# Layer 1 of a four-layer graph network: messages split into a float32r rounding and a remainder, summed by two products per tile

## The reference, cut to what matters

```python
h = jnp.concatenate([x[row], edge_attr], axis=1)
h = jax.nn.relu(h @ W1 + b1) @ W2 + b2
agg = scatter_mean(h, col, dim_size=x.shape[0])
z = jnp.concatenate([x, agg, u[batch]], axis=1)
return jax.nn.relu(z @ W3 + b3) @ W4 + b4
```

## Time and profile before

| | |
|---|---|
| median of three runs | 6288.9 us (6285.21, 6288.9, 6297.36) |
| span of the profiled execution | 6290.0 us; it comes with no time of its own beside the span |
| PE busy over the span | 4549.5 us, 72% |
| DVE, ACT, POOL busy | 2674.4, 1822.6, 3113.1 us |
| gathers of layer 1 | 1612, the first at 873 us, the last at 3245.36 us |

### The profile page before, as it was taken

One profiled execution on the slowest core, in us unless ns is written; L12 is line 12 of the kernel. 1 busy time (PEld: TensorE's weight loads), 2 busy tenths in 40 slices (PEclk: granted clock), 3 DMA queues, 4 the chain that ended last, 5 costly groups with the idle time before them and its releaser, 6 DMA issues.

```text
span 6290.0 us, 72860 instructions
## 1 busy us (share of the span) xinstructions
PE 4549.5 (72%) x24017; PEld 3664.1 (58%) x24017; DVE 2674.4 (43%) x9938; ACT 1822.6 (29%) x3934; POOL 3113.1 (49%) x3324
## 2 busy tenths in 40 slices
PE   6999978888888898888989995344444444544445
PEld 5888855666666566666669994234444343434334
DVE  8999943333333333333335442233333333333334
ACT  5888842222222222222224552011111111111112
POOL 0000036666666666666640004666666666666663
PEclk9999989999999999999999997666666666666667
DMA  6777765555555555555647784122222222222221
GB/s 152 166 163 167 164 162 178 178 179 177 180 176 179 179 177 179 179 179 177 182 133 220 244 243 112 44 48 48 47 47 48 49 48 47 47 50 48 48 48 29
DMA packets 473053, 804.93 MB, mean 128 GB/s; under 512 B 73183, under 2 KB 301706, under 8 KB 462698
## 3 DMA queue, kind: packets, MB, share of 16 engines
q0 software_dynamic: 140192, 443.73, 28.3%
q1 hardware_dynamic: 318378, 346.76, 18.1%
q10 hardware_dynamic: 14112, 9.74, 0.5%
HBM read 663.72 MB, written 136.22 MB: 127 GB/s over the span
## 4 chain that ended last, share of the span: by engine, by line
PE 47%; another core or an unknown queue 25%; DVE 12%; issue 11%; DMA 2%; ACT 2%; POOL 1%; DVEq 0%; ACTq 0%
PE bank L1034 12%; PE bank L1021 10%; PE bank L1205 7%; PE bank L689 5%; PE bank L669 3%; PE bank L1523 2%; DVE ring L987 2%; DVE ring L1415 2%; DMA atab<-at 2%; PE bank L1487 1%; PE bank L590 1%; POOL ring L550 1%; DVE hs L638 1%; PE bank L970 1%
## 5 line engine op out<-in xcount | busy, mean ns | idle before, releaser
L550 POOL DMA_INDIRECT ring<-ptab,src x1612 | 1526.9, 947 | 854.7 <-issue 446.2
L550 POOL DMA_INDIRECT ring<-htab,src x1612 | 1526.5, 947 | 853.1 <-issue 448.3
L1034 PE MATMUL bank<-ring,oh 128*126 128x384 f32 x3224 | 1257.8, 506 | 30.8 <-issue 30.3
L987 DVE TENSOR_TENSOR ring<-bank,ring 128x512 f32<-128x512 f32 x806 | 543.0, 687 | 1613.4 <-remote 855.2
L1021 PE MATMUL bank<-w1e,ea 128*128 128x256 f32 x3224 | 892.4, 400 | 252.2 <-DVE ring L987 190.9
L1021 PEld LDWEIGHTS bank<-w1e,ea 128*128 128x128 f32 x3224 | 620.1, 199 | 541.1 <-issue 270.9
L1523 PE MATMUL bank<-ring,oh 128*126 128x132 f32 x3224 | 675.6, 357 | 337.0 <-DVE ring L1415 224.6
L1003 ACT ACTIVATE ring<-ring 128x1024 f32<-128x1024 f32 x403 | 425.6, 1056 | 1400.5 <-DVE ring L987 1112.6
L1523 PEld LDWEIGHTS bank<-ring,oh 128*126 128x126 f32 x3224 | 583.5, 252 | 424.0 <-issue 219.9
L1034 PEld LDWEIGHTS bank<-ring,oh 128*126 128x126 f32 x3224 | 624.7, 196 | 290.5 <-issue 74.8
L689 PE MATMUL bank<-xhl,at 128*126 128x258 f32 x3822 | 712.6, 323 | 0.0
(11 more groups left out here) (268 smaller groups left out, 4727.0 us busy)
## 6 DMA issues: line engine op xcount, KB each, us to landing
atab<-at POOLq DMA_DIRECT2D x78, 1543.5 KB, 9.9
ring<-ea_r SPq DMA_DIRECT2D x403, 256.0 KB
ea<-ea_t SPq DMA_DIRECT2D x403, 256.0 KB
adjb<-atab SPq DMA_DIRECT2D x156, 535.5 KB, 4.6
adjb<-atab SPq DMA_DIRECT2D x78, 472.5 KB, 4.5
ring<-ptab,src POOLq DMA_INDIRECT x1612
ring<-htab,src POOLq DMA_INDIRECT x1612
ptab<-pO ACTq DMA_DIRECT2D x49, 128.0 KB, 7.3
```

The lines of the kernel that those rows point to most:

```text
L550: return e.indirect_dma_start(o, None, table, bass.IndirectOffsetOnAxis(ap=src[:, t:t + 1], axis=0))
L987: e.tensor_tensor(group1(gi, m % 2), MLP[m % 3][:, :].rearrange("p (g f) -> p g f", g=2), group1(gi, m % 2), ALU.add).then_inc(s_edge, 1)
L1034: w = e.matmul(SUM[s % 2][0:SL, 0:384], slots_of(s, i), rv1[:, t // G % NR1, t % G, :], start=i == 0, stop=t == END[s])
```

## The change

Between ACT's relu and PE's sums stands a new double buffer `halves1` (two groups of 4 x 2 x 384, float32r). ACT writes the relu of the group's rows into its first half, rounded to float32r by the write, and then copies the attributes the same way (`rows_high`, two instructions; it waits for `s_sum1` of group `gi - 2`, which frees the buffer). DVE then writes the remainders: `max(row, 0)` minus the rounding over 128x1024, and attributes minus rounding over 128x512 (`rows_rest`, at `q = 4 gi + 10`). PE sums each tile by two float32r products of 384 columns, with the same stationary slots (now written as float32r). The gathered ring is no longer read by PE: POOL and SP wait for DVE's second remainder (`s_rest1`) instead of `s_sum1`, and the ring has six groups instead of nine. At the end of a set ACT writes the rounding straight from the bank and DVE one subtraction, instead of ACT's scaling and DVE's three steps. The other edits move tensors: layer 3's ring and layer 0's `at0` get places of their own, and `oh` is declared float32r and read as float32 where it was.

```diff
-    NR1 = 9
+    NR1 = 6
+    NH1 = 2
     NR3 = 4
-    RING = max(NR3 * GT * HROW, NR1 * G * 384)
...
+            rv1 = sb("ring1", [P, NR1, G, 384], c=l1)
             ea = sb("ea", [P, NEA, G, P], c=l1)
+            halves1 = sb("halves1", [P, NH1, G, 2, 384], FR, c=l1)
             held1 = sb("held1", [P, NK, 2, 384], FR, c=l1)
-            over1 = sb("over1", [P, 2, 384], c=l1)
...
                 for gi in range(NG):
                     if gi >= NR1:
-                        e.wait_ge(s_sum1, G * (gi - NR1 + 1))
+                        e.wait_ge(s_rest1, 2 * (gi - NR1 + 1))
                     for j in range(G):
...
-            def sums_scaled(e, s):
+            def sums_upper(e, s):
                 e.wait_ge(s_sum1, END[s] + 1)
-                if s >= 2:
-                    e.wait_ge(s_kept1, 3 * s - 4)
-                e.activation(over1[0:SL, s % 2, :], SUM[s % 2][0:SL, 0:384], ACT.Copy, bias=0.0, scale=SPLIT).then_inc(
-                    s_scaled1, 1)
-
-            def sums_kept(e, s):
-
-                o, u, hi, lo = SUM[s % 2][0:SL, 0:384], over1[0:SL, s % 2, :], held1[0:SL, s % NK, 0, :], held1[0:SL, s % NK, 1, :]
-                e.wait_ge(s_scaled1, s + 1)
-                e.tensor_tensor(u, u, o, ALU.subtract).then_inc(s_kept1, 1)
-                e.wait_ge(s_kept1, 3 * s + 1)
                 if s >= NK:
                     e.wait_ge(s_add1, B1[s - NK] + 1)
-                e.scalar_tensor_tensor(out=hi, in0=o, scalar=SPLIT, in1=u, op0=ALU.mult, op1=ALU.subtract).then_inc(s_kept1, 1)
-                e.wait_ge(s_kept1, 3 * s + 2)
-                e.tensor_tensor(lo, o, hi.bitcast(F32), ALU.subtract).then_inc(s_kept1, 1)
+                e.activation(held1[0:SL, s % NK, 0, :], SUM[s % 2][0:SL, 0:384], ACT.Copy).then_inc(s_upper1, 1)
+
+            def sums_kept(e, s):
+
+                e.wait_ge(s_upper1, s + 1)
+                e.tensor_tensor(held1[0:SL, s % NK, 1, :], SUM[s % 2][0:SL, 0:384], held1[0:SL, s % NK, 0, :].bitcast(F32),
+                                ALU.subtract).then_inc(s_kept1, 1)
...
+            def halves_of(gi, h):
+                return halves1[:, gi % NH1, :, h, 0:256], halves1[:, gi % NH1, :, h, 256:384]
+
+            def rows_high(e, gi):
+
+                v, r = halves_of(gi, 0)
+                e.wait_ge(s_edge, 2 * gi + 2)
+                if gi >= NH1:
+                    e.wait_ge(s_sum1, G * (gi - NH1 + 1))
+                e.activation(v, group1(gi), ACT.Relu).then_inc(s_high1, 1)
+                e.wait_ge(s_ea[gi % NR1], 16 * (gi // NR1 + 1))
+                e.activation(r, rv1[:, gi % NR1, :, 256:384], ACT.Copy).then_inc(s_high1, 1)
+
+            def rows_rest(e, gi):
+
+                (v, r), (vh, rh) = halves_of(gi, 1), halves_of(gi, 0)
+                e.wait_ge(s_high1, 2 * gi + 1)
+                e.scalar_tensor_tensor(out=v, in0=group1(gi), scalar=0.0, in1=vh.bitcast(F32), op0=ALU.max,
+                                       op1=ALU.subtract).then_inc(s_rest1, 1)
+                e.wait_ge(s_high1, 2 * gi + 2)
+                e.tensor_tensor(r, rv1[:, gi % NR1, :, 256:384], rh.bitcast(F32), ALU.subtract).then_inc(s_rest1, 1)
...
+                    gi = q // G - 2
+                    if 0 <= gi < NG and q % G == 2:
+                        rows_rest(e, gi)
...
-                        e.wait_ge(s_edge, 2 * gi + 2)
-                        e.activation(group1(gi), group1(gi), ACT.Relu).then_inc(s_relu, 1)
+                        rows_high(e, gi)
                     if q in KEEPS1:
-                        sums_scaled(e, KEEPS1[q])
+                        sums_upper(e, KEEPS1[q])
...
-                            e.wait_ge(s_relu, t // G + 1)
-                            e.wait_ge(s_ea[t // G % NR1], 16 * (t // G // NR1 + 1))
+                            e.wait_ge(s_rest1, 2 * (t // G) + 2)
                         if i == 0:
                             e.wait_ge(s_oh1, s + 1)
                             if s >= 2:
-                                e.wait_ge(s_kept1, 3 * (s - 1))
-                        w = e.matmul(SUM[s % 2][0:SL, 0:384], slots_of(s, i), rv1[:, t // G % NR1, t % G, :], start=i == 0,
-                                     stop=t == END[s])
+                                e.wait_ge(s_kept1, s - 1)
+                        for h in range(2):
+                            w = e.matmul(SUM[s % 2][0:SL, 0:384], slots_r(s, i), halves1[:, t // G % NH1, t % G, h, :],
+                                         start=i == 0 and h == 0, stop=t == END[s] and h == 1)
```

More of the change, by code:

```diff
@@ L229, in slots_of, with slots_r @@
         def slots_of(s, i):
+            return ohf[:, s % 2, SL * i:SL * i + SL]
+        def slots_r(s, i):
             return oh[:, s % 2, SL * i:SL * i + SL]
@@ L491, in expected @@
             s_ptab, s_htab, s_out = (sem(f"s_{n}") for n in ("ptab", "htab", "out"))
-            s_mlp, s_edge, s_relu = (sem(f"s_{n}") for n in ("mlp", "edge", "relu"))
+            s_mlp, s_edge, s_high1, s_rest1 = (sem(f"s_{n}") for n in ("mlp", "edge", "high1", "rest1"))
             l1 = ExitStack()
+            rv1 = sb("ring1", [P, NR1, G, 384], c=l1)
             ea = sb("ea", [P, NEA, G, P], c=l1)
+            halves1 = sb("halves1", [P, NH1, G, 2, 384], FR, c=l1)
             held1 = sb("held1", [P, NK, 2, 384], FR, c=l1)
-            over1 = sb("over1", [P, 2, 384], c=l1)
             l1.close()
@@ L528, in expected @@
             halves2.close()
-            def view(n, w):
-                return ring[:, 0:n * G * w].rearrange("p (n g f) -> p n g f", n=n, g=G)
-            rv1 = view(NR1, 384)
             hbf = hflat.bitcast(BF)
@@ L1538, in any_order @@
             D.sem_inc(s_tick, 16)
+            ring = sb("ring", [P, 2320])
             one = Serial(s_tick, s_own, s_idle)
```

22 lines of the change are left out of this document (11 added, 11 removed).

## The result

The kernel after takes 6452.7 us (median of four runs, 6441.8 to 6459.15) against 6293.13 us for the kernel before on the same chip (four runs, 6285.21 to 6299.78): ratio 1.0252, 95% interval [1.0235, 1.0269]. It is slower, by half of what was forecast (+160 us against +300). The profiled execution has a span of 6455.9 us.

A forecast was written before the change was run, and what follows sets the result against it. Layer 1 was taken as bound by POOL's gathers and their pauses for PE's held increments, not by PE. 6290.0 + 323 (pauses) - 22 (fill and drain) = 6591, given as 6590 us; range 6260 to 6780.

The forecast's parts named there:

- POOL and held increments bound layer 1, not PE: Layer 1: PE's increments are held while gathers run; POOL's pauses, 153 of 2.50 us, let them out.
- The change of credit is what costs: Layer 1's ring: POOL waiting for DVE's second remainder lengthens its pauses; the term that counts, +323 us.
- DVE must first do the edge add (0.69), the two remainders (1.20 + 0.69): Layer 1: DVE's work between held increments' arrival and POOL's restart, at least 2.6 us more per pause.
- I take the middle of the first two, +323 us: Layer 1 pauses: between bursts staying at 9.9 gathers (+421 us) and growing to 13.3 (+225 us), both with the short chain.
- grow in full: Layer 1, short chain: bursts reach 13.3 gathers, 121 pauses of 4.79 us, +225 us.
- POOL is stopped by remainders: Layer 1 rival: gathers stand still 1.20 us per group; 7070 us, half hidden 6830; chance 0.12 shared with slow clock.
- likeliest case: Whole kernel: the forecast's main case, slower at 6590 us, own range 6490 to 6720, chance 0.62.
- Faster rival, float32 passes: Layer 1: holding is tied to PE's float32 passes, so fewer free the increments; 5913 us, chance 0.14 whole or in part.
- PE's sums 0.3 us per tile: PE's sums in layer 1: estimated cadence gain of 0.3 us per tile, valued at nothing in the steady state.
- ACT's new wait for the sums of group gi - 2, "nothing": ACT in layer 1: the wait is on a held increment, but due earlier than the `s_mlp` it stands behind; nothing.
- Fill and drain, -22: Start and end of layer 1: ring of six ends the first stream earlier, -12 us; cheaper sums after last gather, -10 us.
- Layers 0, 2, 3 and DVE's load: nothing: Moved tensors add no instruction in layers 0, 2, 3, 0 us; DVE, some 1370 of 2240 us busy, is no bound.

The follow-up runs named there:

- e4: Kernel after with layer 1's gathers replaced by contiguous loads from SP, so rows are of wrong sources; 5402.3 us (one run).
- e7: Kernel before with layer 1's gathers replaced by contiguous loads from SP, so rows are of wrong sources; 5839.1 us (one run).
- e8: Kernel after with PE summing only the rounded half by one float32 product, remainders made but not summed; 6472.1 us, ratio 1.0277.
- e9: Kernel after with POOL and SP waiting for PE's sums of group gi - 6 instead of DVE's second remainder; 6313.1 us, ratio 1.0034.
- e13: Kernel after with remainders replaced by one-input reductions behind the same waits, PE summing the rounding alone; 6532.0 us, ratio 1.0364.
- e5: Kernel before plus one DVE instruction per group reading two SBUF inputs, that nothing waits for; 6295.0 us, ratio 1.0008.
- e15: Kernel after without making or summing remainders, POOL and SP waiting for PE's sums of group gi - 6; 6256.0 us, ratio 0.9935.
- e6: Kernel before plus one DVE reduction per group reading one SBUF input, that nothing waits for; 6297.5 us, ratio 1.0018.
- e2: Kernel after with the first remainder as a plain tensor_tensor subtraction without the maximum, wrong for negative rows; 6441.9 us, ratio 1.0236.
- e3: Kernel after with relu in place, one rounding copy and one subtraction, each of 4 x 384 columns; 6372.9 us, ratio 1.0134.

## Why the prediction was right, and where its size was off

- *POOL and held increments bound layer 1, not PE:* right. Without gathers no increment is late and PE binds (e4, e7); with them 437 us of PE's work shrink to 20 us (e8).
- *The change of credit is what costs:* right. One edit takes back 87% of the loss (e9). POOL's pauses are released by DVE's second remainder, as forecast, and went from 2.50 to 5.65 us; forecast was 2.50 + 2.6 = 5.1.
- *"DVE must first do the edge add (0.69), the two remainders (1.20 + 0.69)":* the wrong link. The increment that is waited for is not the edge add's `s_mlp` but the sums' `s_sum1`, at ACT's new wait, in all 55 pauses. Behind it stand relu and remainders, 3.19 us, and 2.50 + 3.19 = 5.7 us is the pause that was measured.
- *The term that was mis-sized:* "I take the middle of the first two, +323 us", bursts of 9.9 to 13.3 gathers. Measured, the bursts of the kernel after hold 1392 / 55 = 25 gathers, and pauses cost 0.212 us per gather against 0.219 before: (0.212 - 0.219) x 1612 = -11 us in place of +323. Without stops the chain has bursts of 13.5 (e13), close to the "grow in full" end of 13.3, and costs (0.378 - 0.219) x 1612 = +256 us, near that end's +225. The rest of the growth, from 13.5 to 25, goes with the stops (e13 against the kernel after; e5 shows the same exchange at a smaller size).
- *Rival "POOL is stopped by remainders":* its mechanism is true and its sign wrong. Of at most 1.20 us per group 4 x (1.063 - 0.947) = 0.46 us is lost, 0.116 x 1612 = +187 us. It was to be added to the chain (6830 to 7070 us); in fact it takes more off the pauses than it costs, 6452.7 against 6532.0 us in e13. (In e13 PE's sums are shorter too; by e8 and e15 that is worth 20 to 40 us in favour of e13, so it does not make the difference.) The rows read before could not show it: that gather starts at 2002.39, after the comparison's end at 2002.33. But the trace of the kernel before could: between 1000 and 3200 us 14 gathers start inside a comparison of line 564, and 6 of them last 1.01 to 1.04 us and end 0.82 us after it (one starts at 1638.90, the comparison ends at 1639.12, the gather at 1639.94). The sum -11 + 187 = +176 agrees with the 166 us of the trace.
- *The number:* +160 lies in the range, but by luck in part. The forecast put all of its +300 on pauses, whose price did not rise; what the kernel after lost stands in the length of its gathers, which the sum left out. The likeliest case's own range, 6490 to 6720 us, was missed.
- *Faster rival, float32 passes:* fallen. The sums are float32r, the attribute products aren't, and increments are held in the kernel after too (8.17 and 16.14 us above). With neither kernel free of float32 products, a kernel wholly without them was not tried.
- *PE's sums 0.3 us per tile:* right where PE binds (0.27 us, e4 and e7). *Clock well under 0.95:* right, 0.81; what it costs by itself no run isolates, and e8, at 0.91 and with longer sums, is no faster. *PE's busy share near 60%:* wrong, 1605.60 / 2240 = 72%: the sums keep PE busy for 869.2 / 2833 = 0.307 us per record, not 0.25, and the attribute products for 863.8 / 2834 = 0.305 us where it was 838.1 / 3043 = 0.275. (Single records last 424 ns on average and overlap in time.)
- *ACT's new wait for the sums of group gi - 2, "nothing":* wrong. It was held to be "due earlier than the `s_mlp` that it stands behind", but in PE's program the last sum of group `gi - 2` is at `q` = 4 gi + 7 and the second attribute products of group `gi` at `q` = 4 gi + 2. It stands behind most of the relu's idle time, 834.7 + 374.1 us, where before it was the edge add's increment, 1017.0 us, and it is where every pause of POOL begins to end. Where POOL's credit does not stand behind it, it costs little: e9 keeps it, at 1.0034. With a third group in `halves1` the wait would be for older sums; that was not tried, so its price is open.
- *Fill and drain, -22:* the drain's 10 us are not seen: from the last gather to the end it is 3044.6 us before and 3045.3 after. The fill lies inside the stretch compared and was not read apart.
- *Layers 0, 2, 3 and DVE's load: nothing.* Right; e6 puts the DVE work of half the remainders into the kernel before for 1.0018, at the edge of what can be told apart.

The Trainium skill, "TensorE: Matmul & The Clock Gate", The cost: per-tile semaphore tail, gives 56 ns for an increment; without gathers the traces agree (adds on time), with gathers they don't. The Trainium skill, "SBUF — State Buffer", Who interferes with whom: a DVE instruction with two SBUF inputs contends with a GpSimd instruction that reads SBUF. The traces agree: 267 of 301 gathers that start inside a first remainder last over 1.0 us, none of the 236 that start inside the one-input reduction in its place in e13.

## What to carry to other kernels

When an engine that starts gathers waits for credit, let it wait for a delayed increment itself, not for work that can only begin after one: the same kernel takes 6313 us with PE's increment and 6453 us with DVE's. To see which increment a chain hangs on, count groups on each engine: the one that arrives next to it in time (the add at 2037.43) need not be the one. A cheaper product is worth its time only where the trace without the suspected bound says so (437 us without gathers, 20 us with). And two losses of the same engine's time need not add: before summing a stop and a pause, ask whether one takes the place of the other.

## What the runs showed of the hardware that was not expected

- A gather that starts while DVE reads two SBUF tensors ends 0.82 us after that instruction (median), whatever its form: 1.22 us scalar_tensor_tensor, tensor_tensor of the same size (e2), 1.75 us tensor_tensor (e3), 0.95 us in e5, and 0.28 us in the kernel before where it is long enough to show. Only about 0.12 us of its 0.947 us is done meanwhile.
- One input of that length stops nothing: 1.22 and 0.94 us reductions, gathers 948 and 946 ns (e13, e6).
- PE's increments are held while gathers run, whether the sums are float32 or float32r, and not when contiguous loads from SP bring as many rows (e7: no edge add over 0.46 us late). Stops take the place of pauses: 129 pauses for 1487 gathers with stops, 149 for 1493 without. What holds the increments, and whether a stop lets them out, no run shows.
